# Prologue of a transformer block on one core: split weight loads, v projections last, low parts on GpSimd, q and k rows stored as three terms

## What is computed

```
q, k = rope(x Wq^T + bq) * 16**-0.5, rope(x Wk^T + bk)      # 16 heads of 16
attn = softmax(q k^T) (x Wv^T + bv)
x = layernorm(x + attn Wo^T + bo)
x = layernorm(x + relu(x T(W1)^T + b1) T(W2)^T + b2)        # T: weights to -1, 0, 1 by their mean absolute value
```

## Time and profile before

| | us |
|---|---|
| median of 3 runs | 3211.1 (3210.11 to 3212.7) |
| the profiled execution, its own time | 3212.25 |
| its span in the trace | 3210.4 |
| PE (TensorE) busy | 3166.9 (99%) |
| DVE (VectorE) busy | 2976.6 (93%) |
| ACT (ScalarE) busy | 2519.1 (78%) |
| POOL (GpSimd) busy | 2267.1 (71%) |
| DMA engines' mean busy share, q1 | 45.7% |

### The profile page before, as it was taken

How to read it: one execution, slowest core, us unless ns; L and a number is a source line. 1 busy time by engine, 2 the same in 40 slices (tenths; PEclk the granted TensorE clock), 3 DMA queues, 4 the chain that set the end, 5 groups by cost and what they waited for, 6 DMA issues and landing times.

```text
span 3210.4 us, 83071 instructions
## 1 busy us (share of the span) xinstructions
PE 3166.9 (99%) x31382; PEld 1757.9 (55%) x31382; DVE 2976.6 (93%) x5711; ACT 2519.1 (78%) x4960; POOL 2267.1 (71%) x2582
## 2 busy tenths in 40 slices
PE   6999999999999999999999999999999999999998
PEld 4445555555555555555555555555555555554555
DVE  7999999999999999999999999999999999999995
ACT  3888887888887888878878878878788788778775
POOL 2686876876867767767768768768768677675556
PEclk7999999999999999999999999999999999999999
DMA  8555445355355454453454453553553544543411
GB/s 212 119 106 116 98 106 120 89 112 118 92 116 112 96 118 108 97 120 99 105 120 102 104 119 96 108 121 86 115 116 94 116 111 98 117 101 82 99 52 49
DMA packets 312716, 342.08 MB, mean 107 GB/s; under 512 B 77372, under 2 KB 259964, under 8 KB 312316
## 3 DMA queue, kind: packets, MB, share of 16 engines
q1 hardware_dynamic: 311740, 335.97, 45.7%
q10 hardware_dynamic: 576, 0.79, 0.2%
HBM read 196.41 MB, written 140.24 MB: 105 GB/s over the span
## 4 chain that ended last, share of the span: by engine, by line
PE 96%; DVE 1%; ACT 1%; DMA 1%; issue 1%; POOL 0%; SPq 0%; ACTq 0%; POOLq 0%; DVEq 0%
PE ob L1127 31%; PE sc L1109 27%; PE job L860 25%; PE ms L1094 11%; ACT prob L1276 1%; PE job L912 0%; PE job L1109 0%; DVE mxp L1455 0%; DVE mxp L1708 0%; PE sc L860 0%; DMA qa<-qk_parts 0%; SPq L552 0%; DMA os_<-wv 0%; POOL hid_r L1885 0%; DMA qk_parts<-parts 0%
## 5 line engine op out<-in xcount | busy, mean ns | idle before, releaser
L1455 DVE TENSOR_REDUCE mxp<-ms 128x1 f32<-128x512 f32 x4036 | 2583.8, 681 | 170.4 <-PE ms L1094 140.3
L1276 ACT ACTIVATE prob<-sc 128x512 f32<-128x512 f32 x4034 | 2193.8, 598 | 579.5 <-PE sc L1109 551.6
L1094 PE MATMUL ms<-ka,qa 48*128 48x512 f32 x4036 | 1468.9, 435 | 3.0 <-DVE mxp L1708 2.2
L1109 PE MATMUL sc<-qa,ka 50*128 50x512 f32 x4034 | 1456.6, 432 | 5.2 <-ACT prob L1276 4.1
L1109 PEld LDWEIGHTS sc<-qa,ka 50*128 50x128 f32 x4034 | 680.2, 184 | 1006.8 <-ACT prob L1276 845.2
L1127 PE MATMUL ob<-prob,v_sb 128*17 128x512 f32 (+1 forms) x8304 | 1080.7, 592 | 1.5 <-ACT at_st L1283 1.1
L1094 PEld LDWEIGHTS ms<-ka,qa 48*128 48x128 f32 x4036 | 685.0, 184 | 9.8 <-DVE mxp L1455 5.8
L480 POOL TENSOR_TENSOR rot<-ev_sb,cs_sb 128x512 f32<-128x512 f32 x60 | 77.1, 1285 | 601.8 <-DVE ev_sb L1496 592.7
L1850 POOL TENSOR_TENSOR hid_r<-hid,hid_r 128x512 fp32r<-128x512 f32 x248 | 319.1, 1287 | 19.9
L1127 PEld LDWEIGHTS ob<-prob,v_sb 128*17 128x17 f32 x8304 | 137.7, 95 | 303.1 <-issue 296.4
L860 PEld LDWEIGHTS job<-h_t,w_sb 64*128 64x128 f32 x3968 | 270.2, 185 | 16.6 <-issue 1.1
(11 more groups left out here) (266 smaller groups left out, 3001.4 us busy)
## 6 DMA issues: line engine op xcount, KB each, us to landing
qk_parts<-parts SPq DMA_DIRECT2D x122, 512.0 KB, 4.3
ka<-qk_parts SPq DMA_DIRECT2D x378, 128.0 KB, 4.6
qa<-qk_parts SPq DMA_DIRECT2D x378, 128.0 KB, 7.5
attention<-at_st SPq DMA_DIRECT2D x127, 256.0 KB, 3.0
v_sb<-v_ones SPq DMA_DIRECT2D x68, 272.0 KB, 8.8
v_ones<-v_st SPq DMA_DIRECT2D x64, 272.0 KB, 2.4
xn<-x SPq DMA_DIRECT2D x63, 256.0 KB, 9.1
out<-y SPq DMA_DIRECT2D x63, 256.0 KB, 3.0
```

What stands on the lines that cost most here:

```text
L1094: nc.tensor.matmul(maximum_bank(upto(b, g, NS1, at))[:, :], operand(qa, b, unit_, j, ROWS)[:, qt * P:(qt + 1) * P], operand(ka, b, unit_, ...
L1109: nc.tensor.matmul(score_bank(upto(b, g, HG * STEPS, n))[:, :], operand(ka, b, unit_, head, ROWS + MROWS)[:, tt * P:(tt + 1) * P], operand ...
L1276: nc.scalar.activation(prob[st_ % 2][:, head_at(b, g, st_, j), :], score_bank(upto(b, g, HG * STEPS, n))[:, :], ACT.Exp).then_inc(s["exp_d ...
L1455: nc.vector.reduce_max(mxp[(b * G + g) % 2][:, kh, j * TT + qt:j * TT + qt + 1], maximum_bank(upto(b, g, NS1, at))[:, :], AX.X).then_inc(s ...
```

## The change

- The q, k weights come in two transfers (even, odd), rounded and split as each lands. The v weights are waited for by themselves. The first quarter of the rope table is a transfer of its own, ahead of x of quarter 1.
- TensorE does e and o of all four quarters, then v of all four, into four different staging buffers and banks. ScalarE takes v after the rope work.
- GpSimd takes all four low parts of x and the low parts of the roped quarters 0 to 2; VectorE keeps the last. GpSimd sets two rows of ones first and the other six behind this work.
- `qk_terms` in DRAM holds all three terms. A store is now two DMAs a side: `two_parts_out` (high and low) and `high_again` (the high part once more). `load_side` is two DMAs of 48 partitions a side.
- SP stores and reloads the second rows before it stores v of quarters 1 to 3 and the other heads' rows. The two small products stand behind all 32 tiles.

```
-Q_PARTS = [0, 0, 1]
-K_PARTS = [0, 1, 0]
+TWO_PARTS = ((1, 3), (0, 2))
+HIGH_AGAIN = (0, 2)
+SIDE_STORES = 2
...
+        first_values = [v_st, *(part[:, :, :, :].rearrange("p (g t) h c -> p g t h c", t=TL) for part in v_sb), v_st]
+        first_value_banks = [ms, job, sc, ms]
...
+        QK_DMAS = 2 * 2
+        STORED = 16 * 2 * SIDE_STORES
...
         def load_side(queue, i, b, g, tokens, loaded):
-                for n, a in enumerate(order):
-                    base = half * UPPER + n * HD
-                    queue.dma_start(ring[slot_of(b, g)][base:base + HD, :, tokens].bitcast(fp32), rows[half, a][:, :, tokens]
-                                    ).then_inc(loaded, 16)
+                base = half * UPPER
+                queue.dma_start(ring[base:base + ROWS, :, tokens].bitcast(fp32), rows[half][:, :, tokens]).then_inc(loaded, 16)
...
+            def two_parts_out(b, g, begin, end, stored):
+                for i in range(2):
+                    first, last = TWO_PARTS[i]
+                    sp.dma_start(terms_of(b, i, g, begin, end)[:, :, first:last, :],
+                                 (parts if b else first_parts[g])[begin:end, i].bitcast(fp32)).then_inc(stored, 16)
+            def high_again(b, g, begin, end, stored):
+                for i in range(2):
+                    sp.dma_start(terms_of(b, i, g, begin, end)[:, :, HIGH_AGAIN[i], :],
+                                 (parts if b else first_parts[g])[begin:end, i, :, 0, :].bitcast(fp32)).then_inc(stored, 16)
...
+            for e in range(2):
+                sp.dma_start(raw[:, e], wqk[:, :, :, e, :]).then_inc(s[("even_loaded", "odd_loaded")[e]], 16)
+            sp.dma_start(bqk_sb[:, :, :], bqk).then_inc(s["bias_loaded"], 16)
+            sp.dma_start(wv_raw.rearrange("p (c f) -> p c f", c=KC), wv.rearrange("(c p) f -> p c f", p=P)).then_inc(s["values_loaded"], 16)
+            sp.dma_start(cs_sb[:, :, 0:TQ], rope[:, :, 1, 0:TQ]).then_inc(s["first_rope"], 16)
             first_in(1)
...
+            first_high_out(0, P)
+            parts_out(0, 0)
+            first_high_out(1, P // G)
+            first_heads_out(1)
             v_out(0, 0)
             sp.wait_ge(s["rows_set"], 2)
             for at in range(2):
                 sp.wait_ge(first_stored[at], STORED)
             load_side(sp, 1, 0, 0, slice(0, NQ), s["first_rows"])
             for at in range(2, G):
+                first_high_out(at, P // G)
+                first_heads_out(at)
+            for at in range(2, G):
+                sp.wait_ge(first_stored[at], STORED)
             load_side(sp, 1, 0, 0, slice(NQ, S), qk_loaded[0])
+            sp.wait_ge(s["v_stored"], 16)
+            for at in range(1, G):
+                v_out(0, at)
+            for at in range(1, G):
+                first_rest_out(at)
```

On TensorE:

```
             for g in range(G):
+                for n, kind in enumerate(("e", "o")):
+                    pe.wait_ge(s["weights_low"], n + 1)
                     frees[kind] = whole(proj_job, 0, g, kind, frees[kind], first_r[g], first_banks[kind])
+            for g in range(G):
+                whole(proj_job, 0, g, "v", value_frees[g], first_r[g], first_value_banks[g])
```

On ScalarE:

```
             for g in range(G):
+                proj_job(0, g, "e1", (0, 1), first_banks["e"])
+                if g < 2:
+                    split_first(g + 2)
+                proj_job(0, g, "o1", (0, 1), first_banks["o"])
+                if g > 0:
+                    round_first(g - 1)
+            proj_job(0, 0, "v1", (0, 1), first_value_banks[0])
             round_first(G - 1)
+            proj_job(0, 1, "v1", (0, 1), first_value_banks[1])
+            for at in range(2):
+                act.wait_ge(first_stored[at], STORED)
+            load_side(act, 0, 0, 0, slice(0, NQ), s["first_rows"])
```

On GpSimd:

```
+            for i in range(2):
+                set_rows(i)
+            for g in range(G):
+                split_first(g)
+            for g in range(G - 1):
+                first_low(pool, nc.gpsimd, g)
+            pool.wait_ge(s["parts_done"], G - 1)
+            for i in range(2, 2 * RING + 2):
+                set_rows(i)
```

More of the change, by code:

```diff
@@ L538, in parts_out @@
             def parts_out(b, g):
                 sp.wait_ge(s["parts_done"], upto(b, g, 1, 1))
[L540 to L544, removed]
+                two_parts_out(b, g, 0, P, s["parts_stored"] if b else first_stored[g])
@@ L546, in first_heads_out, with first_high_out @@
+                if b:
+                    high_again(b, g, 0, P, s["parts_stored"])
+            def first_high_out(g, end):
+                sp.wait_ge(s["first_high"], g + 1)
+                high_again(0, g, 0, end, first_stored[g])
             def first_heads_out(g):
                 sp.wait_ge(s["parts_done"], g + 1)
[L548 to L553, removed]
+                two_parts_out(0, g, 0, P // G, first_stored[g])
@@ L1195, in _ @@
                     pe.wait_ge(qk_loaded[0], loads_of(0, 0))
-                if i == HALF_TILES // 2 + len(free_banks):
-                    pe.wait_ge(s["abs_summed"], 2)
-                    nc.tensor.matmul(job[0][:, 0:2], ones[:, :], asum[:, :], start=True, stop=True).then_inc(s["sums_ready"], 1)
-                    pe.wait_ge(s["consts_loaded"], 96)
-                    pe.wait_ge(s["bias_spread"], KC)
-                    for c in range(KC):
-                        last = nc.tensor.matmul(job[1][:, 0:D], y2[:, c, 0:P], wo_sb[:, c, :], start=(c == 0), stop=(c == KC - 1))
-                    last.then_inc(s["bias_ready"], 1)
                 wait_used(pe, s["s1_taken"], i + 1 - len(free_banks))
@@ L1208, in _ @@
                                  ).then_inc(s["s1_ready"], 1)
+            pe.wait_ge(s["abs_summed"], 2)
+            nc.tensor.matmul(job[0][:, 0:2], ones[:, :], asum[:, :], start=True, stop=True).then_inc(s["sums_ready"], 1)
+            pe.wait_ge(s["consts_loaded"], 96)
+            pe.wait_ge(s["bias_spread"], KC)
+            for c in range(KC):
+                last = nc.tensor.matmul(job[1][:, 0:D], y2[:, c, 0:P], wo_sb[:, c, :], start=(c == 0), stop=(c == KC - 1))
+            last.then_inc(s["bias_ready"], 1)
             pe.wait_ge(s["s1_taken"], HALF_TILES)
```

142 lines of the change are left out of this document (59 added, 83 removed).

## The result

The kernel after took 3217.84 us (median of 18 runs, 3216.22 to 3219.6), the kernel before 3212.01 (18 runs, 3210.11 to 3214.53): ratio 1.0017, 95% interval [1.0011, 1.0024]. It is slower by 5.8 us, just under the 0.2% that the prediction called what can be told, but outside its range, which ended at 3215.5. The profiled execution took 3218.35, its span 3216.4, against a span of 3210.4 before. The first scores come at 78.01 instead of 72.16, 5.9 later; the span is 6.0 longer. So the whole loss lies ahead of them.

A forecast was written before the change was run, and what follows sets the result against it. TensorE, idle 0.4 us in 2000, was taken to bound the middle, leaving only the prologue: first scores at 70.7 instead of 72.16, span 3210.4 - 1.5 = 3208.9, median 3209.6 us, range 3201.5 to 3215.5.

The forecast's parts named there:

- Start: Prologue's beginning: TensorE starts at 6.6, 1.9 us earlier, and the odd rows are taken at 13.0 instead of 14.71.
- The ports: Rope, four quarters: each GpSimd operation holds VectorE about 1.2 us at their shared port; last sum at 36.0.
- The rival that the ports don't turn: Rope: VectorE slips between GpSimd's operations, last sum at 28.65, first scores near 63.4, a gain of 8.8 us; chance 0.25.
- First rows: Loading the first q and k rows: q's loads issued at 37.9 to 38.9, first tile at 41.9 against 41.40.
- Tiles: The 32 tiles before the first scores: no wait for second rows, end at 62.1, 2.7 us earlier.
- The maxima's way: Maxima through DRAM before the first scores: store lands at 68.8, load at 70.7, 1.5 us earlier.
- The stores' end: Stores put off, ahead of the maxima in SP's queue: begin at 46.8, take 11.7 us, landed at 59.
- The loads' rate: Row loads of 48 partitions ahead of the maxima: 220 GB/s, between bounds 129 and 364, so 7.0 us.
- the rival that held it: Stores and loads queued ahead of the maxima decide if they drain after 69.6: loss of 7.7 us, 3218.8; chance 0.12.
- What the first scores gain the kernel gains: After the prologue: all later work follows the first scores at TensorE's pace, so their 1.5 us comes off the span.
- The steady part: Middle of the kernel: fewer loads and 512 KB more a unit cost nothing; PE idle stays 0.4 us in 2000.
- The clock: TensorE's granted clock in the prologue: falls in both kernels, as TensorE waits from 33 to 41.9; costed at nothing.

The follow-up runs named there:

- run 3: Kernel after with the low parts of roped quarters 0 to 2 back on VectorE: 3214.28 us.
- run 12: Kernel after with x of batch 1 loaded ahead of the stores put off: 3218.2 us.
- runs 3 to 5: Kernel after with low parts back on VectorE (3214.28 us), with two stored parts and twelve loads of 16 partitions again (3216.69), and with both (3212.48).
- 13: As 9, but W1 and W2 loaded ahead of the second maxima, rows of (0,2) still behind them: 3207.16 us.
- 14: Kernel after with all its own parts and SP's queue in the order of 13: 3209.7 us.
- 1: Kernel after with the maxima of unit (0,0) sent through DRAM ahead of the loads of v and rows for (0,1): 3217.72 us.
- 8: Kernel after, low parts on VectorE, two parts; next x ahead of stores put off, first maxima ahead of (0,1) loads, W1 and W2 behind second maxima: 3211.42 us.
- 9: As 8, with the rows of (0,2) also loaded behind the second maxima: 3210.96 us.
- 10: Kernel after with all its own parts and SP's queue in the order of 9: 3212.82 us.
- 11: Kernel before with only SP's queue put in the order of 9: 3214.75 us.
- run 2: Kernel after with the maxima of unit (0,0) stored and reloaded on ScalarE's DMA queue, SP's loads unchanged: 3228.52 us.
- run 7: Kernel after with the row loads of (0,1) on two queues at once, lower partitions on SP, upper on ScalarE's: 3215.42 us.

## Why the prediction was wrong, by its steps

**Start: right in its time, not in its steps.** TensorE at 6.96 for 6.6. The even half of the weights was rounded from 5.50 on, where 4.75 had been taken, and VectorE's low part began at 6.17, behind GpSimd's split (over at 5.99). So the meeting that set the 6.6 didn't take place, and the later weights set nearly the same time. One sentence failed: that x of quarter 2 "has the same bytes ahead of it now". It came at 14.32 for 11.96 before, so the odd rows were taken at 14.86 and not at 13.0, and the last rope sum is 1.8 later than forecast. From 6 to 10 the engines moved 194 and 261 GB/s in the kernel after, where from 4 to 10 they had moved 344, 339 and 294 before. From 6 to 8 they were busy for only 0.67 of the time (1.01 before), and SP, with two more DMAs ahead, issued the load of that x at 5.60 instead of 3.92. So SP's issuing is the likely cause. Neither it nor the shorter runs of the halved weights was tried.

**The ports: right.** The sums of the four quarters end at 18.8, 26.0, 31.9 and 37.8, so the quarters take 7.2, 5.9 and 6.0; the prediction had 7.25, 6.05 and 6.05. Each meeting costs VectorE 0.95 to 1.1 (1.64 to 1.80 for 0.69), forecast 1.2, and run 3 shows what the low parts on GpSimd cost the kernel: 3.6 us. The rival that the ports don't turn is out.

**First rows: right in the time, by luck.** q's loads went out at 37.91 (forecast 37.9). But the last sum was 1.8 late (37.8 for 36.0), and the 1.86 for rounding it and for v of quarter 1 weren't in the way:

```profile
37.85 0.63 ACT L1332 ACTIVATE parts<-hid 128x512 fp32r<-128x512 f32 x1 [4.26 <-DVE hid L1726]
38.39 0.61 ACT L1332 ACTIVATE parts<-hid 128x512 fp32r<-128x512 f32 x1
38.91 0.64 ACT L1348 ACTIVATE v_sb<-job 128x256 f32<-128x256 f32 x2
```

The ScalarE queue issued the loads 0.09 behind the sum, before ScalarE had rounded it or taken the v that stands ahead of them in the program. In run 3 it is the same (sum over at 34.14, loads at 34.25). The two errors cancel.

**Tiles: right.** First tile 42.39 (41.9), no gap, tiles over at 62.4 (62.1).

**The maxima's way: wrong, in two terms of the sum.** This is the step that failed.
- *The stores' end.* "The stores begin at 46.8 [...] and take 4272 / 364 = 11.7; landed 59": the wait for them ended at 63.1. The rate of 364 was right once they had the engines (383), but up to 50 these moved only 179 to 199 GB/s, with SP's first stores out from 44.44 on and the second rows' loads of 48 partitions still among them. That slow load had been costed for the tiles alone, where it is hidden, and not for the stores behind it. 4.1 us. (x of batch 1, 256 KB, stands in the same queue and wasn't counted either, but behind the stores; with it ahead of them, in run 12, the wait ended at 63.50.)
- *The loads' rate.* 220 GB/s was taken for 48 partitions; 158 to 164 was measured, hardly more than the 145 to 166 at which 16 partitions went at the same place before (60 to 68); the same loads of 48 partitions made 168 to 178 in run 3. 1536 KB at 160 take 9.6 and not 7.0. 2.6 us. The value lay inside the bounds, but at their wrong end; the middle between two bounds by partition count was no measurement.
- Both together are 6.7 of the 7.4 by which the maxima landed later, at 76.2 instead of 68.8; the scores came at 78.01 instead of 70.7. Beside the kernel before, only the first of the two shows: the stores end 6.1 later, the loads take as long. Undoing the low parts on GpSimd brings 2.7 of that back, undoing the three terms 3.7, both 6.1 (runs 3 to 5). The condition "decides when the loads drain after 69.6" was the right condition; the rival that held it, with 0.12, is what happened. It had been priced with the stores and the rows each at their slowest as two separate mishaps. They are one: the slow rows are in the queue twice, ahead of the stores and behind them. The 16.4 us that it gave the stores is what they took (46.8 to 63.1), though not at a rate of 261 throughout.

**"What the first scores gain the kernel gains": half right.** It held for the loss (5.9 at the scores, 6.0 in the span) and in 13 and 14. It failed in 1, 8, 9 and 10, where a lead of 3 to 7 us was gone within 70 us (that of 1.7 in 11 is too near the scatter of the traces to count): a lead brings the next small transfer ahead of the backlog's end. Run 13 shows that this was the order and not a want of DMA time, since it moves the same bytes.

**The steady part: right.** 1999.63 of 2000 busy, the change's larger traffic there (116 GB/s for 106) costs nothing.

**The clock: in part.** "The clock falls in both, as TensorE waits from 33 to 41.9" took the projections to end near 33. They end at 38.2, as v stands behind all the rope work, and the clock fell twice: near 27, and behind 40.

Left open: why x of quarter 2 is late; why the maxima on a queue of their own waited even for later loads (run 2); whether run 7 gains by the halves or by the queue; and how much of the 2.5 us between 13 and 14 each of the two undone parts still makes up in that order.

## What to carry to other kernels

Ask of a small transfer on the critical path not only what stands ahead of it in its own queue, but how many bytes all queues have given to the DMA engines when it is issued, and right behind it, and at what rate these drain; slow loads over few partitions count for all that comes behind them. When a bottleneck is moved forward, follow the same kind of transfer through its next two or three turns before the gain is counted. Put bulk that nobody wants soon into a stretch in which the DMA share is near zero, not simply later.

## What the runs showed of the hardware that wasn't expected

- 16 KB of maxima need 2.5 to 2.7 us from issue until the next step when the engines are free, and 6.2 to 11.0 in SP's queue behind 1.8 MB of loads or more (3.9 where most of them were through, in the kernel before). A queue of their own didn't help: 12.3 (run 2).
- The ScalarE queue issued q's loads without waiting for the ScalarE operations that stand ahead of them in the program: at 37.91, with the rounding over at 39.0 (in run 3 at 34.25, with the rounding over at 35.3).
- Three times the partitions of one half in one load hardly raise the rate (158 to 178 GB/s for 48, 129 to 166 for three loads of 16 side by side), while both halves from two queues give 221 to 236.
- The granted clock fell to half, 1.2 GHz, already from 28 to 30 in the kernel after, behind a stretch in which TensorE was busy for 0.29 of 2 us, and was full again from 34 to 36; it cost nothing there, as VectorE set the pace.
